# Full 128-row transposes in place of pairs of 64-row transposes, in the local-attention layers of a fused kernel

## The chip, the cores and the metric

The kernel runs on one core of a Trainium2 chip. The metric is the device time of one execution in microseconds (us), the median over several runs. The trace is that of one profiled execution.

## What is computed

A latent attention block (8 query heads, 2 key/value heads) is applied to the layer-normalised input (2 sequences, 1024 tokens, 128 features) and added to it. Then six layers follow. Each has windowed attention with 16 heads of 64 features and windows of 32 tokens that look one window back, and then a gated feed-forward part. The windowed part is the one that the change touches:

```python
def attn_layer(x, Wqkv, qs, ksc, Wo):
    qkv = x @ Wqkv
    q, k, v = ...                                # 16 heads x 64
    q = l2norm(q) * qs
    k = l2norm(k) * ksc
    q = q * cos * scale + rotate_half(q) * sin * scale
    k = k * cos * inv + rotate_half(k) * sin * inv
    out = local_attention(q, k, v)               # window 32, keys of 2 windows, softmax
    return out.reshape(b, n, INNER) @ Wo
```

## The kernel before

The tokens are worked on in tiles of 128, so there are 16 tiles to a layer and 96 in all. A long Python loop over steps G writes the instructions of every engine in order; step G handles different stages of several tiles (a software pipeline written out by hand). Engines synchronise with semaphores (`k_nrm`, `kT_mm`, `kT_cp` and so on), and a bank of PSUM is taken again only when its last reader has reported (`claim`, `freed`). The latent block runs first, in about the first 355 us; the six layers take the rest.

In one step TensorE (PE) does, in this order: `weigh` (L1419, attention output, 128x32 array tiles), `values_lower` (L1395, 128x32 tiles), `ln_rows`, `project_queries` (L1141), `ln_columns` (L1450, one 128x128 transpose), `transpose_queries`, `values_upper` (L1395), a piece of the feed-forward part in each step (`up_gate`, `up_value` or `down`, L1141), `transpose_probs`, in one step of four each a further `up_value` or `up_gate`, `scores` (L1380, 64x32 tiles), `project_keys` (L1141), in one step of four `layer_columns` (L1496, four 128x128 transposes), and `transpose_keys`.

The function `transposes` (L1339 to L1345) is called three times per tile: for the keys (`kc`), for the queries (`qc`) and for the probabilities (`prob`). Its source is 128 tokens by 1024 columns. It turns the source in 8 blocks of 128 columns, and each block in two halves of 64 tokens: half o lies in rows 64*o to 64*o+63 of the array, is loaded as weights (64 rows by 128 columns) and multiplied by a 64x64 identity. The half o of all blocks goes to PSUM bank 2+o, 64 columns to a block. ScalarE (ACT) then copies both banks to SBUF with an access pattern (`halves`) that puts the two halves of each block beside each other: `copy_keys` (L722), `copy_queries_T` (L729) and `copy_probs` (L735), each 128x1024.

After `mask_scores` (L755 on ACT), which waits for ACT's copies of the values (L740), `scores` may write its banks. `up_gate` of part 2 waits for VectorE (DVE) to have read bank 6 (`gated`, L1092). GpSimd (POOL) scales the keys (L530), the queries (L536) and the probabilities (L471) ahead of the transposes.

Of the kernel before, what the change touches and what calls it, by code (L numbers as in the profile page):

```python
# [20 lines left out]
ACT = mybir.ActivationFunctionType  # L21
# [3 lines left out]
P = 128  # L25
# [8 lines left out]
DEPTH, LH, LD, WIN = 6, 16, 64, 32  # L34
HALF = LD // 2
HD = LH * LD
NP = LH // 2
# [60 lines left out]
def build(nc, x, wqT, wkdT, wvd, wku, wvuT, wo, wqk, wvo, w1, w2, par, sca, cst_d, tab_d, out):  # L98
    ctx = ExitStack()
    with ctx:  # L100
# [3 lines left out]
        def sem(name):  # L104
            return ctx.enter_context(nc.semaphore(name))
# [26 lines left out]
        ident = cst[:, C_ID:C_ID + P]  # L132
# [24 lines left out]
        kT = arena[:, 0:1280].rearrange("p (k t) -> p k t", k=NP)  # L157
        qT = arena[:, 1280:2304].rearrange("p (k t) -> p k t", k=NP)
        kc, ks, qc, qs = (arena[:, 2304 + HD * i:2304 + HD * (i + 1)] for i in range(4))
        sqk, sqq = (arena[:, 6400 + HD * i:6400 + HD * (i + 1)] for i in range(2))  # L160
        ptile = arena[:, 8448:9472].rearrange("p (k t) -> p k t", k=NP)
# [33 lines left out]
        def bk(i):  # L195
            return banks[:, 512 * i:512 * i + 512]

        def two(i):
            return banks[:, 512 * i:512 * i + 1024]


        def halves(i):

            return two(i).rearrange("p (o k t) -> p k o t", o=2, k=NP)

        counted = {
            "pe": "ln_xT kk_mm m_mm va_mm wvo_mm lq_mm ls_mm lt_mm ly_mm lo_mm".split(),
# [4 lines left out]
        s = {n: sem(n) for v in counted.values() for n in v}  # L212
# [20 lines left out]
        def after(eng, name, n):  # L233

            if n > 0:
                eng.wait_ge(s[name], n)
# [7 lines left out]
        def is_tile(G):  # L244
            return 0 <= G <= LAST_TILE
# [330 lines left out]
        def _(act):  # L576
# [141 lines left out]
            def copy_keys(k):  # L718
                if is_tile(k):
                    act.wait_ge(s["kT_mm"], k + 1)  # L720
                    act.wait_ge(s["look"], k + 1)
                    act.activation(kT[:, :, WIN:WIN + P].rearrange("p k (o t) -> p k o t", o=2), halves(2), ACT.Copy)\  # L722
                       .then_inc(s["kT_cp"], 1)

            def copy_queries_T(k):
                if is_tile(k):
                    act.wait_ge(s["qT_mm"], k + 1)
                    after(act, "s_mm", k)
                    act.activation(qT.rearrange("p k (o t) -> p k o t", o=2), halves(2), ACT.Copy).then_inc(s["qT_cp"], 1)  # L729

            def copy_probs(k):
                if is_tile(k):
                    act.wait_ge(s["pt_mm"], k + 1)
                    after(act, "o_mm", k)
                    act.activation(ptile.rearrange("p k (o t) -> p k o t", o=2), halves(2), ACT.Copy).then_inc(s["pt_cp"], 1)  # L735

            def copy_values(k, g):
                act.wait_ge(s[f"v_mm{g}"], k + 1)
# [97 lines left out]
            for G in range(STEPS):  # L836
                next_key_upper(G)
                gelu(chunk_at(G, 10), 0)
                if G:
                    square_keys(G)  # L840
                last_outputs(G)
                gelu(chunk_at(G, 10), 1)
                copy_layer(chunk_at(G, 13))
                shifted_upper(chunk_at(G, 13))
                exponentials(G - 2)
                copy_keys(G - 1)
                copy_values_lower(G - 1)
                copy_rows(G - 4)
                square_queries(G)
                copy_columns(G - 5)  # L850
                copy_queries_T(G - 1)
                copy_values_upper(G - 1)
                next_folded_lower(G - 1)
                mask_scores(G - 1)
                roots(G)
                next_query_upper(G)
                next_w1_upper(ahead_at(G, 12))
                copy_probs(G - 2)
                next_folded_upper(G - 1)
                gelu(chunk_at(G, 10), 2)  # L860
# [277 lines left out]
        def _(pe):  # L1138
            credit(pe, "pe")
            def mm(o, l, r, start=True, stop=True):  # L1140
                return pe.matmul(o, l, r, start=start, stop=stop)  # L1141
# [3 lines left out]
            for kv in range(KV):  # L1145
                ins = mm(bk(3)[:, P * kv:P * kv + P], gwku, gwkdT[:, P * kv:P * kv + P])
            ins.then_inc(s["kk_mm"], 1)
            pe.wait_ge(s["kk_cp"], CR + 1)
            for kv in range(KV):
                for h in range(REP):  # L1150
                    ins = mm(bk(4 + kv)[:, P * h:P * h + P], gwqT[:, kv * REP + h, :], gkk[:, kv, :])
                ins.then_inc(s["m_mm"], 1)
            pe.wait_ge(c_in, 16)
            for g4 in range(TILES // 4):
# [3 lines left out]
                for k in range(4):  # L1158
                    ins = pe.transpose(bk(g4 % 2)[:, P * k:P * k + P], Xt[:, 4 * g4 + k, :], ident)
# [4 lines left out]
            for t in range(TILES):  # L1164
                b, t0 = divmod(t, NT)
                ins = mm(two(6)[:, 2 * LAT * t:2 * LAT * (t + 1)], X[:, b, P * t0:P * (t0 + 1)], gwv)
            ins.then_inc(s["va_mm"], 1)

            for kv in range(KV):
                for h in range(REP):  # L1170
                    ins = mm(bk(2)[32 * h:32 * h + 32, D * kv:D * kv + D], gwvu, gwo[:, kv * REP + h, :])
# [17 lines left out]
            def claim(*which):  # L1189

                for name, n in sorted({freed[i] for i in which if i in freed}):
                    pe.wait_ge(s[name], n)
# [146 lines left out]
            def transposes(src):  # L1339
                claim(2, 3)  # L1340
                for k in range(NP):
                    for o in range(2):
                        r = slice(64 * o, 64 * o + 64)
                        ins = pe.transpose(bk(2 + o)[:, 64 * k:64 * (k + 1)], src[r, P * k:P * (k + 1)], ident[r, r])  # L1344
                return ins  # L1345

            def project_queries(k):
# [5 lines left out]
            def transpose_keys(k):  # L1353
                if is_tile(k):
                    pe.wait_ge(s["k_nrm"], k + 1)
                    transposes(kc).then_inc(s["kT_mm"], 1)
                    freed[2] = freed[3] = ("kT_cp", k + 1)

            def transpose_queries(k):
                if is_tile(k):  # L1360
                    pe.wait_ge(s["q_nrm"], k + 1)
                    transposes(qc).then_inc(s["qT_mm"], 1)
                    freed[2] = freed[3] = ("qT_cp", k + 1)

            def transpose_probs(k):
                if is_tile(k):
                    pe.wait_ge(s["p_nrm"], k + 1)
                    transposes(prob[:, k % 2, :]).then_inc(s["pt_mm"], 1)
                    freed[2] = freed[3] = ("pt_cp", k + 1)
# [209 lines left out]
```

## Time and profile before

| | |
|---|---|
| median of 3 runs | 1900.57 us (1894.8 to 1902.89) |
| the profiled execution's own time | 1902.89 us |
| its span, first to last instruction | 1901.1 us |
| PE busy | 1742.7 us (92%) |
| DVE, ACT, POOL busy | 1578.4, 1398.1, 1397.2 us |
| mean granted TensorE clock | 0.983 of full speed |

Busy time of PE counts a matmul from its start to its modelled end; matmuls overlap, so for the cost of a run of them the distance from start to start is read. "PEld" are the weight loads. Releasers name what an idle engine waited for; "issue" means that the profile shows nothing.

### The profile page before, as it was taken

The numbers are of one execution on the slowest core, as the hardware profiler recorded it, in microseconds if no ns is written. First come the engines' busy times: TensorE is split into PE (matmuls) and PEld (weight loads), VectorE is DVE, ScalarE is ACT, GpSimd is POOL, SyncE is SP. The second block draws the span as 40 slices with busy tenths as digits, with TensorE's granted clock in tenths as the row PEclk, the third lists the DMA queues.
The fourth block names the chain that finished last, engine by engine and source line by source line (L and its number), as shares of the span: only waits on it lengthen the run. The fifth ranks groups of instructions, "written<-read, shape, count | busy, mean of one in ns | idle before, by whom it ended". The sixth has DMA issues, their size and how long they took to land.

```text
span 1901.1 us, 74970 instructions
## 1 busy us (share of the span) xinstructions
PE 1742.7 (92%) x31556; PEld 1185.9 (62%) x31556; DVE 1578.4 (83%) x2292; ACT 1398.1 (74%) x2240; POOL 1397.2 (73%) x1492
## 2 busy tenths in 40 slices
PE   6878788688999989999999999999999999999996
PEld 5756656455666656666666666666666666666664
DVE  5866767688988987998899988998898898989972
ACT  4667667466787776788777877788777877887773
POOL 3423324598889877898889988889887889888871
PEclk9999999999999999999999999999999999999997
DMA  5000000000001000000000010000100000000000
GB/s 180 2 0 0 0 1 2 1 6 3 10 3 50 3 3 14 3 25 28 3 15 3 3 49 3 7 10 3 49 3 3 15 3 3 3 3 3 8 3 17
DMA packets 12470, 25.71 MB, mean 14 GB/s; under 512 B 1856, under 2 KB 9728, under 8 KB 10496
## 3 DMA queue, kind: packets, MB, share of 16 engines
q1 hardware_dynamic: 12160, 21.18, 3.4%
q8 instruction: 243, 3.98, 0.9%
q14 instruction: 67, 0.55, 0.1%
HBM read 20.13 MB, written 1.05 MB: 11 GB/s over the span
## 4 chain that ended last, share of the span: by engine, by line
PE 54%; DVE 11%; issue 8%; ACT 5%; POOL 4%; DVEq 0%; POOLq 0%; ACTq 0%
PE banks L1141 21%; PE banks L1395 13%; PE banks L1419 7%; PE banks L1344 6%; PE banks L1380 5%; DVE arena L1006 2%; DVE lnx L1068 1%; DVE small L1035 1%; ACT arena L740 1%; DVE small L1041 1%; DVE small L1029 1%; DVE arena L1001 1%; ACT banks L755 1%; POOL arena L530 1%; DVE small L1053 1%
## 5 line engine op out<-in xcount | busy, mean ns | idle before, releaser
L1395 PE MATMUL banks<-M,xs 128*32 128x512 f32 x3072 | 367.4, 595 | 0.9 <-DVE prob L1059 0.4
L1001 DVE TENSOR_TENSOR arena<-banks,tabs 128x1024 f32<-128x1024 f32 x192 | 233.9, 1218 | 42.8 <-ACT arena L700 21.8
L476 POOL TENSOR_TENSOR arena<-arena 128x1024 f32<-128x1024 f32 x96 | 229.6, 2391 | 49.3 <-DVE arena L1006 48.4
L740 ACT ACTIVATE arena<-banks 128x1024 f32<-128x1024 f32 x192 | 197.0, 1026 | 69.0 <-PE banks L1395 67.5
L1006 DVE TENSOR_TENSOR arena<-banks,tabs 128x1024 f32<-128x1024 f32 x192 | 233.3, 1215 | 0.0
L481 POOL TENSOR_TENSOR arena<-arena 128x1024 f32<-128x1024 f32 x96 | 228.2, 2377 | 0.0
L471 POOL TENSOR_TENSOR prob<-prob,small 128x1024 f32<-128x1024 f32 x96 | 184.0, 1917 | 30.1 <-DVE small L1043 30.1
L1068 DVE SCALAR_TENSOR_TENSOR lnx<-lns,small 128x128 f32<-128x128 f32 x96 | 174.1, 1813 | 36.9 <-POOL small L524 36.9
L1419 PE MATMUL banks<-arena 128*32 128x128 f32 x6144 | 192.7, 278 | 5.0 <-ACT arena L813 4.2
L396 POOL TENSOR_TENSOR gqs<-arena,cst 128x128 fp32r<-128x128 f32 x112 | 45.3, 404 | 200.5 <-PE banks L1141 170.7
L536 POOL TENSOR_TENSOR arena<-arena,small 128x1024 f32<-128x1024 f32 x96 | 183.0, 1906 | 9.5
L700 ACT ACTIVATE arena<-banks 128x1024 f32<-128x1024 f32 x96 | 98.4, 1025 | 122.8 <-PE banks L1141 122.6
L530 POOL TENSOR_TENSOR arena<-arena,small 128x1024 f32<-128x1024 f32 x96 | 183.0, 1906 | 7.6
L1141 PE MATMUL banks<-qkH,xsH 128*128 128x512 f32 x384 | 175.3, 456 | 12.1 <-DVE arena L1006 11.2
L1380 PE MATMUL banks<-arena 64*32 64x64 f32 x12288 | 146.0, 226 | 35.8 <-issue 20.5
L1419 PEld LDWEIGHTS banks<-arena 128*32 128x32 f32 x6144 | 166.2, 112 | 12.5 <-issue 5.4
L1380 PEld LDWEIGHTS banks<-arena 64*32 64x32 f32 x12288 | 129.6, 105 | 59.9 <-issue 58.2
L1395 PEld LDWEIGHTS banks<-M,xs 128*32 128x32 f32 x3072 | 87.6, 109 | 123.7 <-issue 116.7
L1141 PE MATMUL banks<-qkL,xsH 128*128 128x512 f32 x384 | 154.8, 403 | 3.3 <-issue 3.3
L1141 PE MATMUL banks<-qkH,xsL 128*128 128x512 f32 x384 | 154.7, 403 | 1.0 <-issue 1.0
L1344 PEld LDWEIGHTS banks<-cst,arena 64*128 64x128 f32 x3072 | 112.7, 140 | 65.4 <-issue 42.8
L711 ACT ACTIVATE arena<-banks 128x1024 f32<-128x1024 f32 x96 | 98.5, 1026 | 74.5 <-PE banks L1141 74.5
(128 smaller groups left out, 4167.4 us busy)
## 6 DMA issues: line engine op xcount, KB each, us to landing
arena<-in_wvo_dram SPq DMA_DIRECT2D x6, 1024.0 KB, 5.3
qkraw<-in_wqk_dram SPq DMA_DIRECT2D x6, 1024.0 KB, 4.8
W<-in_w_dram SPq DMA_DIRECT2D x6, 341.0 KB, 2.9
W<-in_w_dram SPq DMA_DIRECT2D x6, 192.0 KB, 2.5
res<-in_x_dram SPq DMA_DIRECT2D x4, 256.0 KB, 3.8
tabc<-in_tab_dram SPq DMA_DIRECT2D x1, 1024.0 KB, 9.6
out_dram<-res SPq DMA_DIRECT2D x4, 256.0 KB, 2.3
sca_s<-in_sca_dram SPq DMA_DIRECT2D x6, 128.0 KB, 2.1
```

Source lines behind the costliest of these rows:

```text
L476: pool.tensor_tensor(kc, kc, ks, ALU.add).then_inc(s["k_add"], 1)
L481: pool.tensor_tensor(qc, qc, qs, ALU.add).then_inc(s["q_add"], 1)
L530: pool.tensor_tensor(heads(kc), heads(kc), over(rs[:, 4, 0:LH], LD), ALU.mult).then_inc(s["k_nrm"], 1)
L740: act.activation(vw[:, (2 * k + g) % RV, :], two(V_BANK), ACT.Copy).then_inc(s[f"v_cp{g}"], 1)
L1001: dve.tensor_tensor(heads(c), heads(two(0)), table(k % NT, kind), ALU.mult).then_inc(s[done], 1)
L1006: dve.tensor_tensor(w.rearrange("p (h z k) -> p h z k", h=LH, z=2), swapped(two(0)), table2(k % NT, kind + 1), ALU.mult).then_inc(s[done], 1)
L1068: dve.scalar_tensor_tensor(lnx[:, :], lns[:, k % 2, :], ag[:, k % 2, 0:1], rs[:, 4, 32:33].to_broadcast([P, D]), ALU.subtract, ALU.mult).t ...
L1141: return pe.matmul(o, l, r, start=start, stop=stop)
L1344: ins = pe.transpose(bk(2 + o)[:, 64 * k:64 * (k + 1)], src[r, P * k:P * (k + 1)], ident[r, r])
L1380: ins = pe.matmul(bk(4 + o)[WIN * w:WIN * (w + 1), 64 * j:64 * (j + 1)], qT[r, j, WIN * w:WIN * (w + 1)], kT[r, j, WIN * w:WIN * w + 64], ...
L1395: ins = pe.matmul(bk(V_BANK + z)[WIN * q:WIN * (q + 1), :], xs[:, b, t0:t0 + WIN], M[:, q, :, :].rearrange("p m n -> p (m n)"), start=True ...
L1419: ins = pe.matmul(bk(PV_BANK)[WIN * w:WIN * (w + 1), 0:D], ptile[:, NQ * z + m, WIN * w:WIN * (w + 1)], block_of(k, w - 1 + z)[:, D * m:D ...
```

## The change

`transposes` turns each block of 128x128 in one piece, with the whole array and the 128x128 identity: 8 instructions in place of 16. Blocks 0 to 3 go to bank 2 and blocks 4 to 7 to bank 3, so the two banks hold the result in its final order, and the three ACT copies read them straight. Nothing else is changed: the order of the work, the semaphores and the sizes stay.

```diff
-        def halves(i):
-
-            return two(i).rearrange("p (o k t) -> p k o t", o=2, k=NP)
...
-                    act.activation(kT[:, :, WIN:WIN + P].rearrange("p k (o t) -> p k o t", o=2), halves(2), ACT.Copy)\
+                    act.activation(kT[:, :, WIN:WIN + P], two(2).rearrange("p (k t) -> p k t", k=NP), ACT.Copy)\
                        .then_inc(s["kT_cp"], 1)
...
-                    act.activation(qT.rearrange("p k (o t) -> p k o t", o=2), halves(2), ACT.Copy).then_inc(s["qT_cp"], 1)
+                    act.activation(qT[:, :, :], two(2).rearrange("p (k t) -> p k t", k=NP), ACT.Copy).then_inc(s["qT_cp"], 1)
...
-                    act.activation(ptile.rearrange("p k (o t) -> p k o t", o=2), halves(2), ACT.Copy).then_inc(s["pt_cp"], 1)
+                    act.activation(ptile[:, :, :], two(2).rearrange("p (k t) -> p k t", k=NP), ACT.Copy).then_inc(s["pt_cp"], 1)
...
             def transposes(src):
                 claim(2, 3)
                 for k in range(NP):
-                    for o in range(2):
-                        r = slice(64 * o, 64 * o + 64)
-                        ins = pe.transpose(bk(2 + o)[:, 64 * k:64 * (k + 1)], src[r, P * k:P * (k + 1)], ident[r, r])
+                    ins = pe.transpose(bk(2 + k // 4)[:, P * (k % 4):P * (k % 4 + 1)], src[:, P * k:P * (k + 1)], ident)
                 return ins
```

## Rows read from the trace of the kernel before

**Rows 1.** The page: busy time, share of the span and instructions of each engine.

```profile
PE 1742.7 (92%) x31556; PEld 1185.9 (62%) x31556; DVE 1578.4 (83%) x2292; ACT 1398.1 (74%) x2240; POOL 1397.2 (73%) x1492
```

**Rows 2.** Busy time by stretch, in the layers: PE, PEld, DVE, ACT, POOL; granted clock, DMA.

```profile
1000.00:1300.00 300.00, 291.57 (x5844) 193.43 (x5841) 270.59 (x314) 237.18 (x342) 260.67 (x249) 0.99 0.04 12
```

**Rows 3.** PE's groups by shape, all of the run.

```profile
L1344 PE MATMUL banks<-cst,arena 64*128 64x64 f32 x3072 | 139.4, 231 | 6.2 <-POOL arena L530 3.6 <-issue 1.9
...
L1496 PE MATMUL banks<-cst,Xt 128*128 128x128 f32 x80 | 12.0, 272 | 0.0
```

**Rows 4.** Timeline of PE, 1108.8 to 1116.9 us: start, length, what, how many.

```profile
1108.87 0.39 PE L1141 MATMUL banks<-qkH,xsL 128*128 128x512 f32 x1
1109.10 0.60 PE L1496 MATMUL banks<-cst,Xt 128*128 128x128 f32 x4
1109.63 0.72 PE L1344 MATMUL banks<-cst,arena 64*128 64x64 f32 x16
1110.27 1.96 PE L1419 MATMUL banks<-arena 128*32 128x128 f32 x64
...
1115.96 0.27 PE L1450 MATMUL banks<-cst,lnx 128*128 128x128 f32 x1
1116.16 0.71 PE L1344 MATMUL banks<-cst,arena 64*128 64x64 f32 x16
1116.80 1.92 PE L1395 MATMUL banks<-M,xs 128*32 128x512 f32 x16
```

**Rows 5.** Timeline of PE: transposes of probabilities and what follows them, four steps.

```profile
1120.25 0.71 PE L1344 MATMUL banks<-cst,prob 64*128 64x64 f32 x16
1121.11 1.13 PE L1380 MATMUL banks<-arena 64*32 64x64 f32 x93 [0.15 <-ACT banks L755]
...
1137.83 0.71 PE L1344 MATMUL banks<-cst,prob 64*128 64x64 f32 x16
1138.84 0.90 PE L1141 MATMUL banks<-xnw,w1w 128*85 128x512 f32 x3 [0.29 <-DVE arena L1092]
...
1152.59 0.71 PE L1344 MATMUL banks<-cst,prob 64*128 64x64 f32 x16
1153.23 0.93 PE L1141 MATMUL banks<-xnw,w1w 128*85 128x512 f32 x3
...
1170.26 0.71 PE L1344 MATMUL banks<-cst,prob 64*128 64x64 f32 x16
1170.90 1.48 PE L1380 MATMUL banks<-arena 64*32 64x64 f32 x128
```

**Rows 6.** Waits, all of the run: in total us, times, longest us.

```profile
PE banks L1380 <- issue: 20.5, 10, 2.5
...
PEld banks L1344 <- POOL arena L530: 20.4, 42, 1.9
...
PEld banks L1344 <- POOL prob L471: 16.3, 25, 2.1
```

**Rows 7.** ACT copies, 1100 to 1400 us: busy us, mean ns of one.

```profile
L740 ACT ACTIVATE arena<-banks 128x1024 f32<-128x1024 f32 x38 | 39.0, 1026 | 11.6 <-PE banks L1395 11.4
...
L735 ACT ACTIVATE arena<-banks 128x1024 f32<-128x1024 f32 x19 | 19.2, 1012 | 4.2 <-PE banks L1344 4.1
```

**Rows 8.** Timeline of PE from 1107.6 and from 1124.3 us: projections at either clock.

```profile
1107.60 0.50 PE L1141 MATMUL banks<-qkH,xsH 128*128 128x512 f32 x1
...
1124.39 0.70 PE L1380 MATMUL banks<-arena 64*32 64x64 f32 x35 [2.15 <-issue]
1125.02 0.80 PE L1141 MATMUL banks<-qkH,xsH 128*128 128x512 f32 x1
...
1127.88 0.75 PE L1344 MATMUL banks<-cst,arena 64*128 64x64 f32 x16
```

**Rows 9.** Busy time by stretch, 1125.00 to 1127.90 us; columns as in rows 2.

```profile
1125.00:1127.90 2.90, 2.90 (x9) 1.85 (x8) 2.45 (x2) 0.00 (x0) 2.75 (x3) 0.50 0.02 6
```

**Rows 10.** DMA queues: packets, MB, share of 16 engines' span.

```profile
q8 instruction: 243, 3.98, 0.9%
```

## The prediction

> **What bounds the kernel now.** I read the busy times first. PE is busy for 92% of the span, nine points more than the next engine [rows 1]. The table by stretch says where the rest is: in a stretch of 300 us in the middle of the layers PE is busy for 291.6 us (97%), DVE for 90%, POOL for 87%, ACT for 79% [rows 2]. The layers take some 1,500 us of the 1,901. PE's busy time is no proof of work, since a matmul counts until its modelled end. So I went on to the timeline of PE and read distances from start to start. There one group begins as soon as the previous one has streamed, over most of a step of about 15.5 us; the idle times in it are few and named [rows 4, 5]. Last I read the waits. Before the transposes the weight loads wait for POOL, 20.4 + 16.3 = 36.7 us over the run, in part behind matmuls that still stream; in the middle of the scores PE waits 20.5 us for nothing that the profile names [rows 6]. The path through the layers is therefore PE's own list of work. What is added to it is added to the time, except ahead of a place where PE waits for another engine anyway.
>
> **The present call.** One call is 16 transposes that run as 8 pairs, one of each pair in the upper and one in the lower half of the array. The group is 0.71 us long and one matmul lasts 0.22 us at the full clock, so the last one starts 0.49 us after the first: 0.07 us for a pair [rows 4]. A call stands between groups of other array shapes. From the single transpose of 128x128 (L1450, 1115.96) to the first pair it is 0.20 us, and from the last pair (1116.16 + 0.49 = 1116.65) to the next shape (1116.80) it is 0.15 us [rows 4]. From L1450 to the values the present call takes 0.84 us.
>
> **The new call.** The trace has the new instruction already, in `layer_columns`: fp32, 128x128, moved against the 128-column identity. Four of them span 0.60 us with 0.272 us for one [rows 3, 4], so they start (0.60 − 0.272)/3 = 0.109 us apart. A whole block takes 0.109 us where a pair takes 0.07: a pair moves only 64 columns of identity through each half of the array at once. Eight blocks start over 7 × 0.109 = 0.76 us, against 0.49 us now. That is +0.27 us.
>
> **The edges of a call.** L1450 and the projections ahead of a call have the 128x128 shape too. The first L1496 starts 0.23 us after a projection, with no more between them than the projection's own 512 columns [rows 4]. So the entry gets shorter: 0.109 in place of 0.20 us, −0.09 us. The exit gets longer: a change of shape behind a 128x128 transpose costs 0.20 us (L1450 to the present call) and behind a pair 0.15 [rows 4], so +0.05 us. For the exit into 128x32 the trace has no such case; I take this nearest one, and the bounds are no change of the exit (0) and +0.09, if the next shape must wait for more of the longer matmul. Sum per call: +0.27 − 0.09 + 0.05 = +0.23 us.
>
> The Trainium skill (TensorEngine Tiling (Array Packing), section Key Properties) says that a change of the tiling mode drains the engine. The trace agrees: 0.20 us to another shape, 0.11 within one [rows 4]. By that rule alone the change gains, since a call that stands beside the 128x128 shape needs one drain less; the rows say that this gain is 0.09 us and that the longer calls cost three times as much.
>
> **Call by call.** Keys: behind them `weigh` (128x32), PE waits for nothing: +0.23. Queries: behind them `values_upper`: +0.23. Both 96 times: 192 × 0.23 = 44.2 us. The probabilities go by the step of four, 24 tiles to each kind [rows 5]:
> - before `scores`, with `down` ahead (1170.26 to 1170.90, 0.64 us, no wait): +0.23.
> - before `up_value` 2 (1152.59 to 1153.23, 0.64 us, no wait): the exit needs no change of shape, 0.109 in place of 0.15. New distance 0.76 + 0.11 = 0.87; less the shorter entry, 0.87 − 0.09 − 0.64 = +0.14.
> - before `up_gate` 2 (1137.83 to 1138.84, 1.01 us): PE waits here for DVE, which works on `up_value` 0, issued ahead of the transposes. The new 0.87 − 0.09 = 0.78 lies below 1.01: 0.
> - before `scores` with both `up_gate` ahead (1120.25 to 1121.11, 0.86 us): the scores wait for ACT's mask, behind ACT's copy of the values. 0.86 − 0.64 = 0.22 us of cover against +0.23: about 0.
>
> That is 24 × (0.23 + 0.14) = 8.9 us. Were the covers gone, it would be 24 × 0.37 = 9 us more. Sum: 44.2 + 8.9 = +53 us. I take off 1 us for the first and last tiles, where PE waits anyway. +52 us.
>
> **The rest of the change.** The ACT copies read the banks in order instead of in halves. The plain copy of the same size takes 1026 ns (L740), the copy with halves 1012 (L735) [rows 7]. So the pattern costs nothing and nothing comes back; ACT is not on the path but at the mask, and 0.01 us × 288 is 3 us at the most. PE's list gets shorter by 8 × 3 × 96 = 2,304 transposes with as many loads, 4,608 instructions. PE has 2 × 31556 of them [rows 1], and one queue brings 3.98 MB of instructions in 243 packets [rows 10]; 63,112 instructions for 3.98 MB are 63 bytes each, so these are PE's. 4,608 fewer are 0.29 MB or 18 packets. In the middle of a run of scores PE stops, 10 times in all, 20.5 us [rows 6]. I read these stops as PE waiting for its instructions. After one of 2.15 us the granted clock is at 0.50, the 1.2 GHz level [rows 8, 9], and the six projections take 2.86 us, against 1.50 at 2.4 GHz (1107.60 to 1109.10) [rows 4, 8]: one stop costs 2.15 + 1.36 = 3.5 us. Where the stops fall after the change depends on where the boundaries of the packets fall, and I can't forecast it. Counted at 0; five stops more or fewer are ±18 us.
>
> **Sum.** The profiled execution took 1902.9 us, so it would take 1955 us. It stands 2.3 us above the median of the runs, and against 1900.6 the forecast is 1952 us, +2.7%. Its own range: 0.18 us per call with the exit at no cost, and 0.27 with the exit at its upper bound, hence +43 and +61, plus 18 us of stops either way taken as independent (the root of 9² + 18² is 20): 1930 to 1974.
>
> **Rivals.**
> - *The stretch is absorbed by waits on POOL.* The weight loads of the transposes wait 36.7 us for POOL in 67 calls [rows 6]. If POOL set the step, a longer PE group would only fill these waits: 52 − 37 = +15 us, 1916. For it: POOL is busy for 87%. Against it: POOL has 2 us free in each step, and in the timeline PE goes into most calls with no wait. Fully absorbed would be no change, 1901. The first 6 in 100, the second 3.
> - *The loads set the pace in both forms (faster).* Each pair needs two loads of 128 columns, each block one. If the 0.07 us of a pair is what loads of 128 columns take, and the 0.109 us of L1496 came of something else there, a new call starts its 8 blocks over the same 0.49 us. Then a call changes by −0.09 + 0.05 = −0.04 us, or −0.09 with the exit at its lower bound; −12 to −26 us for 288 calls, about 1882. It decides at a pitch of 0.076 us (0.49 + 0.04 over 7): below this the new call is the shorter one. Against it stand 80 transposes of just this kind at 0.109. 3 in 100.
> - *The stops vanish (faster).* With 4,608 fewer instructions all 10 stops would have to go, 35 us, and the calls cost the least, +43: still slower. Only together with absorbed calls does it come out under 1890. 1 in 100.
> - *More stops.* Ten more: 1952 + 35 = 1987. 5 in 100.
>
> The Trainium skill (TensorE: Matmul & The Clock Gate, section LDWEIGHTS) gives columns/1.2 ns for a load, whatever the rows; that would be an estimate of 107 ns for each load in either form, and by it alone the 8 loads of a new call would pace it just as the 8 pairs do today. The rows disagree: pairs start 0.07 us apart, so a load of 128 columns is done in less.
>
> **Chances.** The forecast holds 82 in 100. The range 1928 to 1976 leaves out the absorbed cases (9), the faster ones (4), and most of the many stops (5). A measurement of this kernel can tell about 0.5% from no change, that is 10 us. Slower: 82 + 5 + 6 = 93 in 100. Same: 3. Faster: 4.
>
> **What the profile after would show.** Right, if L1344's successor has 2,304 matmuls of 128x128 with means near 0.272 us, eight of them spanning 7 × 0.109 + 0.27 = 1.03 us; if L1450 to the values is about 1.07 us (0.84 now); if `up_gate` 2 still waits for DVE, but for less; if PE's busy share stays at 92 to 93% while those of DVE, ACT and POOL fall; if the ACT copies stay near 1.02 us. Wrong, if the blocks start 0.07 us apart; if waits on POOL ahead of the transposes shrink by as much as PE's groups grow; if the stops in the scores differ by more than five in number; or if the exit costs far from 0.20 us.

## The result, and the profile after

The changed kernel takes 1929.91 us (median of 4 runs, 1926.84 to 1930.64), the kernel before 1897.68 us on the same chips (4 runs, 1893.11 to 1902.89). The ratio is 1.0166, 95% interval 1.0134 to 1.0199: slower, by 32 us. The forecast was slower, 1952 us with a range of 1928 to 1976; the time lies at the lower end of the range. The profiled execution of the changed kernel has a span of 1928.9 us, 27.8 us more than the one before.

The lines of the source have new numbers: `transposes` is L1338 now, `scores` L1374, `weigh` L1413, the values L1389, the projections L1137, `layer_columns` L1490, `ln_columns` L1444. First the page, busy times by engine, and by stretch (columns as in [rows 2]):

```profile
PE 1794.4 (93%) x29252; PEld 1274.4 (66%) x29252; DVE 1579.7 (82%) x2292; ACT 1397.5 (72%) x2240; POOL 1398.2 (72%) x1492
```

```profile
1000.00:1300.00 300.00, 292.39 (x5248) 205.25 (x5247) 261.52 (x300) 231.66 (x333) 251.57 (x241) 0.99 0.04 12
```

PE has 2,304 matmuls less than in [rows 1] and is busy for 52 us more. DVE, ACT and POOL do the same work to within 1.3 us. In 300 us of the layers ACT and POOL get through less of it (231.7 and 251.6 us, against 237.2 and 260.7 in [rows 2]), since the steps got longer. PE's groups by shape:

```profile
L1338 PE MATMUL banks<-cst,arena 128*128 128x128 f32 x1536 | 202.3, 274 | 4.7 <-POOL arena L526 3.1 <-issue 1.5
L1338 PE MATMUL banks<-cst,prob 128*128 128x128 f32 x768 | 99.9, 272 | 2.0 <-POOL prob L467 2.0
L1490 PE MATMUL banks<-cst,Xt 128*128 128x128 f32 x80 | 12.0, 272 | 0.0
```

The new transposes last what those of `layer_columns` lasted in [rows 3]. The timeline of PE answers to [rows 4] (its first four rows to the keys, the others to the queries) and [rows 5]; the last row is cut short by the end of the view:

```profile
1120.80 0.60 PE L1490 MATMUL banks<-cst,Xt 128*128 128x128 f32 x4
1121.23 1.03 PE L1338 MATMUL banks<-cst,arena 128*128 128x128 f32 x8
1122.20 1.95 PE L1413 MATMUL banks<-arena 128*32 128x128 f32 x64
...
1127.89 0.27 PE L1444 MATMUL banks<-cst,lnx 128*128 128x128 f32 x1
1128.00 1.04 PE L1338 MATMUL banks<-cst,arena 128*128 128x128 f32 x8
1128.97 1.92 PE L1389 MATMUL banks<-M,xs 128*32 128x512 f32 x16
...
1132.33 1.04 PE L1338 MATMUL banks<-cst,prob 128*128 128x128 f32 x8
1133.30 1.48 PE L1374 MATMUL banks<-arena 64*32 64x64 f32 x128
...
1146.59 1.03 PE L1338 MATMUL banks<-cst,prob 128*128 128x128 f32 x8
1147.68 0.90 PE L1137 MATMUL banks<-xnw,w1w 128*85 128x512 f32 x3
...
1161.79 1.03 PE L1338 MATMUL banks<-cst,prob 128*128 128x128 f32 x8
1162.58 0.94 PE L1137 MATMUL banks<-xnw,w1w 128*85 128x512 f32 x3
...
1178.36 1.04 PE L1338 MATMUL banks<-cst,prob 128*128 128x128 f32 x8
1179.32 0.90 PE L1374 MATMUL banks<-arena 64*32 64x64 f32 x68
```

From `ln_columns` to the values it is now 1128.97 − 1127.89 = 1.08 us, against 0.84 before: entry 0.11, then 0.97 to the next shape. That is +0.24, the forecast sum for one call (+0.23) within the 0.01 us of the rows. If PE pays this in 192 calls and the rest as forecast, 52 us should come out, and 28 came in this profile. The waits show where to look (total us, times, longest):

```profile
PE banks L1374 <- issue: 11.9, 7, 2.4
...
PEld banks L1338 <- POOL prob L467: 7.2, 9, 1.7
PEld banks L1338 <- POOL arena L526: 6.3, 7, 1.9
```

Two lines of [rows 6] shrank. The waits of the weight loads on POOL went from 36.7 to 13.5 us, which looks like the first rival. The stops in the middle of the scores went from 20.5 us in 10 to 11.9 us in 7.

**A ledger.** To tell the two apart I took the distances from start to start of all PE's matmuls between 485 us and 48 us before the end, and sorted each into one of four heaps. "Calls" are the distances into, within and out of a transpose call, real waits included. "Stops" is what a distance has over the usual one for that pair of instructions, where PE idled over 0.45 us. "Half clock" is what distances have over the usual ones in stretches with a granted clock of 0.50. "Rest" is the rest. Matmul records that are missing blur a heap by some us.

| us | span | calls | rest | stops | half clock |
|---|---|---|---|---|---|
| before | 1901.1 | 253.7 | 1067.0 | 34.4 | 12.6 |
| changed | 1928.9 | 300.1 | 1069.1 | 22.2 | 4.4 |
| difference | +27.8 | +46.4 | +2.1 | −12.2 | −8.2 |

(What lies outside is 533 us long in both, since the counted part is set by times of the run and not by tiles; −0.3 is rounding and edges. The changed kernel has half a tile more in its counted part. Taken from the scores of tile 8 to those of tile 95, the same work in both, the difference is +19.1 us: calls +48, stops and half clock together −27, rest −2. The forecast for these 87 tiles is 53 × 87/96 = 48.) So the calls cost nearly what was forecast, and 20 us came back from something that the change does not touch in itself: PE stood still less often, and was less often at 1.2 GHz behind it. The waits of the loads on POOL were no cover: PE itself, matmuls and not loads, idled for POOL ahead of its transposes for only 3.6 + 3.0 = 6.6 us over the run before ([rows 3] and the row below) and 5.1 us now, and the calls got longer by the full amount. That is a reading of one pair of profiles, and the experiments test it.

```profile
L1344 PE MATMUL banks<-cst,prob 64*128 64x64 f32 x1536 | 68.2, 229 | 3.2 <-POOL prob L471 3.0
```

**Where the stops lie.** I counted PE's instructions (loads, matmuls, semaphore waits) from the last branch, behind which the list is straight. The stops inside the scores of the kernel before, from 485 us to 1840, come at counts 11828, 13621, 14901, 16180, 23605, 27959, 31028, 41021, 44085 and 58934. Modulo 256 these are 52, 53, 53, 52, 53, 55, 52, 61, 53 and 54. In the changed kernel the four of over 1 us in that stretch are at 52, 57, 59 and 52 modulo 256. A queue brings 3.98 MB in 243 packets [rows 10], 16 KB each; if a packet holds 256 instructions, an instruction has 64 bytes (an estimate from these two numbers). The changed kernel has 4,608 instructions less, which is 18 times 256, and its queue brings 18 packets less:

```profile
q8 instruction: 225, 3.69, 0.8%
```

So a stop comes where PE goes over into the next packet. The scores are 256 instructions in 1.48 us, the densest part of the list.

**What PE waits for there.** The packets themselves are in the trace. In each of the 10 stops of the kernel before, one 16 KB packet of this queue began to load between 1.02 us before PE stood still and 0.07 us after, and PE went on 1.20 to 1.56 us after that packet had landed. For the stop of 2.15 us in [rows 8], PE stands from 1122.23 us, the packet loads from 1122.22 to 1123.18, and PE goes on at 1124.39. Over all 14 builds this holds for 116 of 116 stops of over 1 us in the scores (start −1.40 to +0.26 us, 1.19 to 1.61 us from landing to going on), while the queue loads packets for only 13 to 15% of the time. PE waits for its instructions there; the profile shows it, though its list of waits gives no name.

### The profile page after: what moved, and what is told of

It reads as the page before. It is cut to its first block, busy times and chain, and to the rows that moved or that the text cites. A ratio compares the mean times of both kernels' runs of the same rounds, so it can differ in the third digit from the quotient of the medians.

```text
span 1928.9 us, 70362 instructions
## 1 busy us (share of the span) xinstructions
PE 1794.4 (93%) x29252; PEld 1274.4 (66%) x29252; DVE 1579.7 (82%) x2292; ACT 1397.5 (72%) x2240; POOL 1398.2 (72%) x1492
## 4 chain that ended last, share of the span: by engine, by line
PE 73%; issue 3%; ACT 2%; DVE 1%; POOL 1%; DVEq 0%; ACTq 0%; POOLq 0%
PE banks L1137 27%; PE banks L1389 17%; PE banks L1338 12%; PE banks L1413 9%; PE banks L1374 7%; PE banks L1435 1%; ACT arena L736 1%; PE banks L1444 1%; PE banks L1490 0%; DVE arena L1002 0%; ACT L809 0%; ACT banks L751 0%; POOL arena L526 0%; ACT arena L696 0%; DVE small L1031 0%
## 5 line engine op out<-in xcount | busy, mean ns | idle before, releaser
L1389 PE MATMUL banks<-M,xs 128*32 128x512 f32 x3072 | 367.1, 595 | 0.2 <-DVE prob L1055 0.2
L736 ACT ACTIVATE arena<-banks 128x1024 f32<-128x1024 f32 x192 | 196.8, 1025 | 103.5 <-PE banks L1389 103.3
L1338 PE MATMUL banks<-cst,arena 128*128 128x128 f32 x1536 | 202.3, 274 | 4.7 <-POOL arena L526 3.1
L1338 PEld LDWEIGHTS banks<-cst,arena 128*128 128x128 f32 x1536 | 177.5, 141 | 26.5 <-POOL arena L526 6.3
L1413 PE MATMUL banks<-arena 128*32 128x128 f32 x6144 | 189.8, 276 | 4.1 <-ACT arena L809 3.8
L392 POOL TENSOR_TENSOR gqs<-arena,cst 128x128 fp32r<-128x128 f32 x112 | 45.3, 404 | 201.7 <-PE banks L1137 170.6
L1137 PE MATMUL banks<-qkH,xsH 128*128 128x512 f32 x384 | 173.4, 452 | 12.2 <-DVE arena L1002 9.2
L696 ACT ACTIVATE arena<-banks 128x1024 f32<-128x1024 f32 x96 | 98.4, 1025 | 109.5 <-PE banks L1137 109.3
L1413 PEld LDWEIGHTS banks<-arena 128*32 128x32 f32 x6144 | 163.6, 110 | 21.0 <-issue 20.9
L1389 PEld LDWEIGHTS banks<-M,xs 128*32 128x32 f32 x3072 | 88.0, 109 | 131.5 <-issue 131.5
L1374 PE MATMUL banks<-arena 64*32 64x64 f32 x12288 | 144.1, 226 | 22.8 <-issue 11.9
L1374 PEld LDWEIGHTS banks<-arena 64*32 64x32 f32 x12288 | 127.7, 105 | 51.2 <-issue 51.2
L1137 PE MATMUL banks<-qkL,xsH 128*128 128x512 f32 x384 | 153.1, 399 | 2.5 <-issue 2.5
L1137 PE MATMUL banks<-qkH,xsL 128*128 128x512 f32 x384 | 153.4, 400 | 1.3 <-issue 1.3
```

What stands on the lines that cost most here:

```text
L736: act.activation(vw[:, (2 * k + g) % RV, :], two(V_BANK), ACT.Copy).then_inc(s[f"v_cp{g}"], 1)
L1338: ins = pe.transpose(bk(2 + k // 4)[:, P * (k % 4):P * (k % 4 + 1)], src[:, P * k:P * (k + 1)], ident)
L1374: ins = pe.matmul(bk(4 + o)[WIN * w:WIN * (w + 1), 64 * j:64 * (j + 1)], qT[r, j, WIN * w:WIN * (w + 1)], kT[r, j, WIN * w:WIN * w + 64], ...
L1389: ins = pe.matmul(bk(V_BANK + z)[WIN * q:WIN * (q + 1), :], xs[:, b, t0:t0 + WIN], M[:, q, :, :].rearrange("p m n -> p (m n)"), start=True ...
L1413: ins = pe.matmul(bk(PV_BANK)[WIN * w:WIN * (w + 1), 0:D], ptile[:, NQ * z + m, WIN * w:WIN * (w + 1)], block_of(k, w - 1 + z)[:, D * m:D ...
```

## The experiments

Theory A: a call costs what was forecast, and the rest of the difference comes from where the packet boundaries fall. Theory B: waits on other engines absorb about 40% of what PE is given, and the stops only went along. Theory B', of the last round, says that calls of whole blocks are cheaper than forecast and the stops only went along. All kernels ran against the kernel before on the same chip.

### The parts alone

`transposes` stays, and the new form is added as `whole_transposes`; one kernel uses it for keys and queries, the other for the probabilities. The matching ACT copies change as in the change itself.

```diff
-                    transposes(kc).then_inc(s["kT_mm"], 1)
+                    whole_transposes(kc).then_inc(s["kT_mm"], 1)
...
-                    transposes(qc).then_inc(s["qT_mm"], 1)
+                    whole_transposes(qc).then_inc(s["qT_mm"], 1)
```

> Keys and queries are transposed in whole 128x128 blocks, probabilities stay in pairs of halves. Theory A (the cost of a call is as forecast, and PE's stops for instructions were what changed besides): L1450 to the values 1.07 us and the projections to the next shape 1.20 us, that is +0.23 us on 192 calls, +44 us, less or more what the stops at packet boundaries and the half-clock stretches behind them give: between +25 and +55 us. Theory B (waits on other engines absorb about 40% of what PE is given): +27 us, with the stops of the kernel before unchanged in number and place.

```diff
-                    transposes(prob[:, k % 2, :]).then_inc(s["pt_mm"], 1)
+                    whole_transposes(prob[:, k % 2, :]).then_inc(s["pt_mm"], 1)
```

> Only the probabilities are transposed in whole blocks. Theory A: +9 us from the calls (0.23 us before the scores with down ahead, 0.14 us before up_value 2, nothing where PE waits for DVE or for ACT's mask), and stops at other tiles than before: -10 to +20 us. Theory B: about +5 us with the stops where they were.

Keys and queries: 1933.37 us against 1899.99, ratio 1.0169 (1.0140 to 1.0199). That lies between A's +25 and +55 and is 6 us above B's +27. The ledger has the calls at +40.0 us, stops −5.8 and half clock −3.7. The probabilities: 1930.11 us, ratio 1.0149 (1.0117 to 1.0181), +30 us, which is beyond what either theory gave. The parts cost 33 and 30 us, and together 32. In the ledger the calls of the probabilities cost +8.8 us, close to the 8.9 × 88/96 = 8.2 of the forecast for its part; what was off were the stops, +19.1 us. The waits of that kernel, and one of the stops in its timeline:

```profile
PE banks L1386 <- issue: 44.3, 23, 2.7
```

```profile
1102.77 0.62 PE L1386 MATMUL banks<-arena 64*32 64x64 f32 x40
1105.61 0.51 PE L1386 MATMUL banks<-arena 64*32 64x64 f32 x31 [2.21 <-issue]
1106.04 0.79 PE L1141 MATMUL banks<-qkH,xsH 128*128 128x512 f32 x1
```

23 stops in place of 10, and the first projection behind this one lasts 0.79 us, as the one at half clock in [rows 8] (0.80, against 0.50 at the full clock). All long stops in these scores stand at 52 to 63 modulo 256.

### The same work, moved in the list

```diff
+                    for _ in range(2 if k == 0 else 0):
+                        transposes(kc)
                     transposes(kc).then_inc(s["kT_mm"], 1)
```

With 4 in place of 2 the shift is 128 instructions.

> The kernel before, with the transposes of the first tile's keys written three times over (64 more PE instructions, once, about 1 us of PE at a place where it waits for POOL anyway). All later work is the same, but stands 64 instructions further on in PE's list. Theory A: the long stops in the middle of the scores still come when the count of PE instructions from the last branch is 52 to 61 modulo 256, so they fall on other tiles, and their number changes (5 to 15); the time moves with it by about 3.5 us a stop, up to 15 us either way. Theory B: stops at the same tiles as before and the time the same within 3 us.

> As the shift by 64, with 128 more PE instructions (about 2 us of PE once). Theory A: stops again at counts of 52 to 61 modulo 256, on yet other tiles; the time moves by about 3.5 us for each stop more or fewer. Theory B: the same tiles and the same time within 3 us.

Shifted by 64: 1897.51 us, ratio 0.9979 (0.9949 to 1.0008). By 128: 1904.83 us, 1.0024 (1.0000 to 1.0049). The times moved little: −2.5 us meets theory B's 3 us, and +4.8 us is near it. Theory A had left open up to 15 us, so the times decide little. The places of the stops are not B's. From tile 8 on the long ones in the scores were on tiles 17, 20, 22, 24, 36, 43, 48, 64, 69 and 93; shifted by 64 on 17, 33, 38, 40, 45, 47, 52, 66 and 85; by 128 on 9, 14, 28, 42, 54, 68, 82 and 89. The counts stay at 52 to 61 modulo 256. A shift moves all boundaries alike and leaves their number near 9; it takes other lengths of a step to meet the scores more or less often.

### Steered away from the boundaries, and into them

A table `PAD`, worked out from the counts in the trace of the same kernel without it, says how many groups of 16 filling instructions stand ahead of each tile's value products:

```diff
                     claim(PV_BANK)
+                    for _ in range(PAD.get(k, 0)):
+                        for w in range(NW):
+                            pe.matmul(bk(PV_BANK)[WIN * w:WIN * (w + 1), 0:8], ptile[:, 0, WIN * w:WIN * (w + 1)],
+                                      block_of(k, w - 1)[:, 0:8], start=True, stop=True, skip_group_check=True)
```

> The kernel before with 992 PE instructions of filling, spread over 26 tiles ahead of the value products (small matmuls into columns that the next matmul overwrites). A table says how many groups of 16 stand ahead of each tile, so that the packet boundary (count 52 modulo 256) never falls into the last 56 of the 256 instructions of a tile's scores. Theory A (a stop comes where a packet boundary falls late in the scores): 0 to 3 long stops in the scores in place of 10, less half-clock time; filling costs 3 to 8 us, stops give back 25 to 35 us: 20 to 30 us faster than the kernel before. Theory B (stops have nothing to do with the place in the list): about as many stops, and 3 to 8 us slower.

> The changed kernel with 272 instructions of filling on 9 tiles, steered the same way. Theory A: 0 to 3 long stops in the scores in place of 7; 10 to 20 us faster than the changed kernel, and against the steered kernel before it shows the calls alone: 45 to 55 us slower than it. Theory B: as the changed kernel, and the distance between the two steered kernels stays at about 32 us.

> The kernel before with 2096 instructions of filling on 40 tiles, placed so that the packet boundary falls near instruction 242 of the scores' 256 at as many tiles as up to 112 instructions of filling allow. Theory A: 30 to 42 long stops in the scores and 80 to 130 us slower than the kernel before. Theory B: 10 stops as before, 7 to 15 us slower for the filling.

> Only the probabilities in whole blocks, steered so that no packet boundary falls late in the scores. Theory A: 0 to 3 long stops in place of 22, and against the steered kernel before 5 to 13 us slower, which is the forecast term of the probabilities. Theory B: 30 us slower than the kernel before as without steering.

Measured, in turn: 1879.68 us, ratio 0.9883 (0.9842 to 0.9924); 1910.76, 1.0063 (1.0047 to 1.0079); 1931.72, 1.0164 (1.0122 to 1.0206); 1934.48, 1.0192 (1.0153 to 1.0230). The stops in the scores of the kernel steered into the boundaries, and one of them, then the same row of the changed kernel steered away:

```profile
PE banks L1383 <- issue: 44.1, 32, 2.5
```

```profile
1075.15 1.40 PE L1383 MATMUL banks<-arena 64*32 64x64 f32 x119
1078.48 0.32 PE L1383 MATMUL banks<-arena 64*32 64x64 f32 x9 [1.93 <-issue]
```

```profile
PE banks L1377 <- issue: 2.1, 1, 2.1
```

The place of a boundary in the scores is a cause and not a companion. With the same work but for the filling, the kernel before has 32 stops or 5 in the scores and takes 1932 us or 1880. 11 us of the 52 between them is the difference in filling, at 9 to 10 ns an instruction (the rest of the list grew by 9.2 us for 992 in one and by 20.6 for 2,096 in the other); stops and half-clock time give 36 (table below). The slowdown by steering in, 32 us against the kernel before, was forecast at 80 to 130, and 20.6 us of it are filling: stops and half-clock time together grew by only 9.3. There were fewer stops than thought (32 short and long, 23 of over 1 us), they cost 1.7 us each with half-clock time (44.1 + 11.0 over 32), not 3.5, and with the boundaries in the scores the stops elsewhere went from about 14 us to 1. The two steered kernels stand 31 us apart, which is theory B's number. In the profiled executions they stand 24.6 apart, and the ledger says why it is not 47: the kernel before has 720 instructions more of filling (rest +9.6 us), and it still had 5 stops in the scores and 16 in all, and 1.6 us at half clock, against 8 in all in the changed one (14.8 us less of stops and half clock). The calls alone are 49.1 us longer in the changed one.

The probabilities alone did not get faster, against theory A. Their waits:

```profile
PE banks L1389 <- issue: 44.1, 20, 2.4
```

There are 20 stops where A had 0 to 3. All fell at boundaries 178 to 199 instructions into the scores, right below my limit of 200, where the filling had pushed them. In that kernel PE stops from a lower place on. So I steered again, with the limit at 172.

### With a wider margin, and with little filling

The same edit with other tables: for the kernel before (1,776 instructions of filling), for the changed one (512), for the probabilities alone (1,120), and for the kernel before once more with the limit at 214 (288 instructions on 12 tiles):

```diff
+PAD = {15: 2, 20: 1, 27: 1, 31: 2, 43: 1, 47: 2, 52: 1, 63: 2, 68: 1, 75: 1, 79: 2, 91: 2}
```

> The kernel before, steered with a wider margin: no packet boundary in the last 84 of the scores' 256 instructions (but on every fourth tile, where almost no stop was seen), with 1776 instructions of filling. Theory A: 0 or 1 long stops in the scores; filling costs about 10 ns an instruction, as in the first steered run (992 instructions, rest of the list +9 us), so +18 us, and stops and half-clock time give back 30 to 40: 1875 to 1890 us. Theory B' (the calls of whole blocks are cheaper than forecast, and the stops only went along): the three wide kernels stand as far apart as the unsteered ones (+32 for the change, +30 for the probabilities).

> The changed kernel, steered with the wide margin, 512 instructions of filling (about 5 us). Theory A: 0 or 1 long stops in the scores, and with the filling taken off both (10 ns an instruction) 45 to 55 us above the wide kernel before, the forecast sum. Theory B': about 32 us above it.

> Only the probabilities in whole blocks, steered with the wide margin, 1120 instructions of filling (about 11 us). In the last run all 20 stops fell at boundaries 178 to 199 instructions into the scores, just under the limit of 200. Theory A: with the limit at 172 they go, 0 to 3 stops, and with the filling taken off both the kernel is 5 to 13 us above the wide kernel before. Theory B': still 30 us above the kernel before.

> The kernel before, steered with little filling (288 instructions, 12 tiles), away from the last 42 instructions of the scores only, where 19 of 25 boundaries stopped PE. Theory A: 1 to 5 long stops in the scores, 3 us of filling, 1872 to 1885 us: the fastest kernel. Theory B: no faster than the kernel before.

Measured, in turn: 1886.81 us, ratio 0.9943 (0.9921 to 0.9964); 1914.05, 1.0084 (1.0067 to 1.0101); 1901.71, 1.0011 (0.9989 to 1.0033); 1868.14, 0.9838 (0.9820 to 0.9857). The stops in the scores of the probabilities alone, and of the kernel with little filling:

```profile
PE banks L1389 <- issue: 15.4, 11, 2.5
```

```profile
PE banks L1383 <- issue: 1.1, 3, 0.6
```

The probabilities alone are 33 us faster than steered with the narrower limit, though they carry 688 instructions more of filling; 8 of the 11 stops are still over 1 us, where A had 0 to 3. The kernel before with little filling came out below the forecast 1872 to 1885. All builds in the ledger (fill is the number of filling instructions; stops in the scores are the total and the times of the profile's wait):

| build | median us | fill | stops in the scores | calls | rest | stops | half clock |
|---|---|---|---|---|---|---|---|
| before | 1897.7 to 1900.0 | 0 | 20.5, 10 | 253.7 | 1067.0 | 34.4 | 12.6 |
| before, limit 200 | 1879.7 | 992 | 6.4, 5 | 252.6 | 1076.2 | 18.6 | 1.6 |
| before, limit 172 | 1886.8 | 1776 | 1.0, 3 | 252.5 | 1082.8 | 16.0 | 0 |
| before, limit 214 | 1868.1 | 288 | 1.1, 3 | 254.7 | 1070.1 | 9.5 | 0 |
| before, steered in | 1931.7 | 2096 | 44.1, 32 | 251.4 | 1087.6 | 45.3 | 11.0 |
| changed | 1929.9 | 0 | 11.9, 7 | 300.1 | 1069.1 | 22.2 | 4.4 |
| changed, limit 200 | 1910.8 | 272 | 2.1, 1 | 301.7 | 1066.6 | 5.4 | 0 |
| changed, limit 172 | 1914.1 | 512 | 4.5, 5 | 300.4 | 1071.7 | 10.2 | 0 |
| keys, queries | 1933.4 | 0 | 15.5, 7 | 293.7 | 1067.3 | 28.6 | 8.9 |
| probabilities | 1930.1 | 0 | 44.3, 23 | 262.5 | 1073.6 | 53.5 | 10.6 |
| probabilities, limit 200 | 1934.5 | 432 | 44.1, 20 | 261.9 | 1068.2 | 48.8 | 14.6 |
| probabilities, limit 172 | 1901.7 | 1120 | 15.4, 11 | 260.4 | 1076.0 | 27.2 | 2.8 |

The two builds nearest to each other in filling and almost free of long stops in the scores (none and one) are before with limit 214 and changed with limit 200: 1868.1 and 1910.8 us. Each was timed against the kernel before on its own chip, 0.9838 and 1.0063 of it; that is (1.0063 − 0.9838) × 1900 = 43 us for the change once the stops are out, give or take 5 by the two intervals. With the limit at 172, the filling taken off at 9 ns an instruction, it is 27.2 + 11.4 = 39 us, again give or take 5. Both are below the 45 to 55 expected, though that lies within the first one's interval, and above the 32 us of theory B' (the second by little more than its interval). In each pair the changed kernel still has fewer stops, 4.1 and 5.8 us; with these added back it is 47 and 44 us. For the probabilities alone the same sum gives 1901.7 − 10.1 − (1886.8 − 16.0) = 21 us, above the 5 to 13 expected; 11.2 + 2.8 = 14 us of it are stops and half-clock time that they still have more, so 7 us are left for the calls.

## Why the prediction was right, and what was off

**The pace of the transposes and the edges: right.** Seven starts take 0.76 us (0.109 each), the entry 0.11, the exit into 128x32 0.20, as the nearest rows said. The trace had a run of four of the very same instruction, and the pace held for runs of eight. The rival in which the loads set the pace in both forms is out: 2,304 new transposes at 0.109 us.

**Keys and queries: right.** +40.0 us for the 88 of 96 tiles in the counted part, forecast 192 × 0.23 × 88/96 = 40.5.

**The probabilities: right in the sum, not in each kind.** +8.8 us against 8.2 for the counted tiles. By kind in the timelines, with the entry 0.09 shorter: ahead of the scores with `down` 0.96 − 0.64 − 0.09 = +0.23; ahead of the masked scores 0.97 − 0.86 − 0.09 = +0.02; ahead of `up_gate` 2, 1.09 − 1.01 − 0.09 = 0; ahead of `up_value` 2, 0.79 − 0.64 − 0.09 = +0.06, where I had +0.14. These four give 24 × 0.31 = 7.4 us for all tiles, against 8.9. The projection starts 0.03 us after the last transpose there and not 0.11.

**The first and last tiles: right in size.** I took off 1 us. By tile, the first scores start 1.6 us later in the changed kernel, those of tile 8 8.3 us later, those of tile 95 27.5 us, and the end comes 27.8 us later. In the 8.3 us lies a stop of 2.2 us in the scores of tile 4. From the scores of tile 0 to those of tile 8 the distances into, within and out of calls sum up to 38.7 us before and 41.9 us now: +3.2, where 8 tiles at the forecast 53/96 us each give 4.4. PE's waits ahead of the transposes shrank there from 12.5 to 10.2 us, which covers the rest.

**The step that was off: "counted at 0" for the stops.** The forecast said that stops fall where packet boundaries fall, and gave them ±18 us and no direction. They took off 12.2 us, and the half-clock stretches behind them 8.2. Together that is the whole distance from 46 us of calls to 28 us of span, and it is more than the 18 us that the range had for it. The number in the scores fell by only 3, from 10 to 7. But each cost less: 3.3 us with half-clock time before ((20.5 + 12.6)/10, near the forecast 3.5) and 2.3 us now ((9.7 + 4.4)/6 in the counted part), because two are short and fewer are followed by a half-clock stretch (4 of 7 over the run, against 8 of 10). PE also stops outside the scores (21 and 18 stops of over 0.45 us in all). The calls came out as forecast and the range had this term, so the time lies in the range; that it does so by 2 us, and on which side of 1952, was chance.

**The ACT copies: right.** The plain copy of the values and the copy of the probabilities, which reads the banks in order now (columns as in [rows 7]):

```profile
L736 ACT ACTIVATE arena<-banks 128x1024 f32<-128x1024 f32 x36 | 36.9, 1025 | 18.1 <-PE banks L1389 18.1
...
L731 ACT ACTIVATE arena<-banks 128x1024 f32<-128x1024 f32 x19 | 19.2, 1010 | 5.4 <-PE banks L1338 5.4
```

1010 ns in place of 1012: the order of reading neither costs nor gives.

**Waits on POOL: seen, and no cover.** The loads' waits fell by 23 us while the calls grew by the full amount. PE's own idle time for POOL ahead of the transposes was 6.6 us before and is 5.1 now, so there was almost nothing to absorb.

**What stays open.** The change alone, with the stops in the scores steered away, measures 39 to 43 us where the ledger's calls say 47 (for 88 of 96 tiles) and the forecast 52 for all. Stops outside the scores, which no build was free of, account for 4 to 6 us of the difference to 47; what is then left lies within the intervals. Nor do I know why PE stops from about 166 instructions into the scores on with whole probabilities and mostly from 225 on with halves. The trace shows only that the next packet starts late there (next section), not what holds it back. Nothing was tried that takes the stops away without filling.

## What to carry to other kernels

Price an exchange of instructions by the distance between starts, in a run of the same instruction that the trace already has, plus the way in and the way out; here that gave the calls of keys and queries to 0.01 us, and missed by 0.08 us on one kind of the probabilities. Where an engine is fed from a long straight list, a change of the list's length moves the packet boundaries, and the time with them, here by up to 1 to 2%, whatever the change is about (a shift of the whole list by 64 or 128 instructions moved it by 0.3% at most): two parts that cost 33 and 30 us cost 32 together. Compare versions with the boundaries steered to the same places, or at least read the stops before believing a difference of a per cent; steering alone made the kernel before 1.6% faster (1868.14 us), and this version beats both kernels.

## What the runs showed of the hardware

PE's stops depend on the place of the boundary (count 52 modulo 256) in a tile's scores. Over all builds, tiles 8 to 91 but every fourth, boundaries and stops of over 1 us:

| boundary at instruction | 0 to 159 | 160 to 177 | 178 to 199 | 200 to 224 | 225 to 255 |
|---|---|---|---|---|---|
| halves everywhere (7 builds) | 278, none | 41, none | 38, 6 | 35, 1 | 49, 40 |
| keys and queries whole | 38, none | 4, none | 7, none | 7, 1 | 7, 6 |
| probabilities whole (3 builds) | 127, none | 20, 5 | 27, 22 | 6, 6 | 9, 9 |
| all whole (3 builds) | 158, 1 | 17, none | 2, none | 8, 3 | 4, 1 |

(The place of a boundary is known to within a few instructions.) On every fourth tile, which the table leaves out, there were 8 stops of over 1 us in 294.

Whether PE stops goes by when the next packet of its queue starts to load. Of the boundaries 40 to 248 instructions into the scores, tiles 8 to 91, all builds, PE stood for over 1 us at 97. There the packet began to load at the earliest 1.2 us before PE came to the boundary, or only after it. At the other 876 it had begun at least 1.4 us before. A packet takes about 1.1 us to load (0.9 to 1.5), and PE went on 1.2 to 1.6 us after it had landed. A late start has two forms. A boundary in the last 31 instructions of the scores has the one before it just ahead of them: there PE ran through a whole packet in 1.4 to 3.5 us (under 2.8 in all but three cases) before it stopped. But at the 33 stops with the boundary 160 to 199 instructions into the scores PE had taken 5.1 to 6.0 us for the packet, and the next one began all the same only 0.9 us before its end or later; why isn't shown.

In the kernel before a pair of loads of 64 rows by 128 columns, one for each half of the array, goes every 0.07 us (0.49 us from the first to the last of 8 pairs), so a load of 128 columns holds up the next by no more than that. A change of the array's shape costs about 0.09 us over the stream of the matmul ahead of it (0.20 us from `ln_columns` to the 64-row transposes [rows 4], 0.11 to the 128-row ones). A single execution of the kernel before, with no change at all, varies from 1889.82 to 1908.87 us over 19 runs; the build with almost no stops from 1865.11 to 1868.72 over 4.
